# Four transformer stages on one core: the order of turns, output transposes and depooling statistics in the first attention

## The reference

```
# first attention (16 heads of 8), per batch
Q = heads(LN(x)) * 8 ** -0.5;  K, V = heads(ctx[..., :128]), heads(ctx[..., 128:])
logits = Q @ K.T + b + (-1e12) * invalid
x = x + tanh(g_xattn[0]) * softmax(logits) @ V
...
# depooling of the second layer, from ctx and the patch lengths alone
h_patch = rmsnorm(ctx)[..., :128];  s[t] = a * s[t-1] + bcoef * h_patch[t]
depool_out = s[plug],  plug = clip(cumsum(boundary_mask) - 1, 0, 127)
```

## Time and profile before

| | us |
|---|---|
| median of three runs | 1140.29 (1137.04 to 1141.31) |
| the profiled execution | 1144.96 |
| its span | 1143.6 |
| PE busy in the span | 924.6 (81%) |
| DVE busy | 663.6 (58%) |
| ACT busy | 439.8 (38%) |
| GpSimd busy | 438.5 (38%) |
| mean granted TensorE clock | 0.876 of full |

### The profile page before, as it was taken

How to read it: one execution, slowest core, us unless ns; L and a number is a source line. 1 busy time by engine, 2 the same in 40 slices (tenths; PEclk the granted TensorE clock), 3 DMA queues, 4 the chain that set the end, 5 groups by cost and what they waited for, 6 DMA issues and landing times.

```text
span 1143.6 us, 23576 instructions
## 1 busy us (share of the span) xinstructions
PE 924.6 (81%) x8435; PEld 736.0 (64%) x8435; DVE 663.6 (58%) x1745; ACT 439.8 (38%) x864; POOL 438.5 (38%) x718
## 2 busy tenths in 40 slices
PE   2867795999982988995777859999577878888898
PEld 2545674888872766774556648888546666666565
DVE  3787644776775555433354525756655776642655
ACT  0444534333322232330444315566404454554312
POOL 5444444443620544325465443647233453100100
PEclk9999757999995999997899659999756999996999
DMA  5321112121213000002122111123111010000262
GB/s 173 103 52 53 56 48 85 37 43 48 65 41 104 14 12 12 1 1 67 57 71 67 34 26 47 43 59 77 33 33 39 25 27 21 13 7 29 74 192 86
DMA packets 51310, 59.34 MB, mean 52 GB/s; under 512 B 7456, under 2 KB 36928, under 8 KB 50816
## 3 DMA queue, kind: packets, MB, share of 16 engines
q1 hardware_dynamic: 45776, 46.44, 13.7%
q0 software_dynamic: 4992, 10.23, 4.1%
q10 hardware_dynamic: 432, 1.18, 0.3%
HBM read 42.81 MB, written 9.24 MB: 46 GB/s over the span
## 4 chain that ended last, share of the span: by engine, by line
PE 59%; DVE 19%; issue 6%; DMA 6%; POOL 4%; ACT 3%; SPq 2%; POOLq 0%; DVEq 0%; ACTq 0%
PE banks L412 9%; DVE NM L482 6%; PE banks L420 4%; PE bank L181 4%; PE banks L175 3%; PE banks L176 3%; PE banks L177 3%; PE banks L1805 3%; PE bank L433 3%; PE bank L2227 3%; PE banks L1806 3%; PE banks L1807 3%; PE banks L1808 3%; PE bank L2118 2%; DMA QT<-NMT 2%
## 5 line engine op out<-in xcount | busy, mean ns | idle before, releaser
L412 PE MATMUL banks<-KT,QT 31*128 31x128 f32 (+1 forms) x1280 | 158.4, 381 | 90.9 <-DVE NM L482 43.6
L482 DVE TENSOR_REDUCE NM<-banks 128x4 f32<-128x1024 f32 (+1 forms) x112 | 136.7, 1221 | 141.3 <-PE banks L412 141.2
L412 PEld LDWEIGHTS banks<-KT,QT 31*128 31x128 f32 x1280 | 111.0, 219 | 123.6 <-DVE NM L482 53.2
L456 ACT ACTIVATE EE<-banks 128x1024 f32<-128x1024 f32 x112 | 114.8, 1025 | 191.9 <-PE banks L420 191.9
L420 PE MATMUL banks<-QT,KT 32*128 32x128 f32 x1792 | 157.4, 319 | 2.9 <-ACT EE L456 2.5
L420 PEld LDWEIGHTS banks<-QT,KT 32*128 32x128 f32 x1792 | 130.0, 216 | 7.9 <-issue 6.6
L1737 POOL DMA_INDIRECT XG<-xn,SL x92 | 89.4, 972 | 103.5 <-PE bank L1775 84.4
L433 PE MATMUL bank<-EE,VV 128*32 128x128 f32 x1792 | 73.5, 311 | 0.8 <-ACT EE L456 0.8
L1874 ACT ACTIVATE ONE<-CP,EC 128x128 fp32r<-128x128 f32 x92 | 37.0, 403 | 81.1 <-PE bank L2057 56.9
L433 PEld LDWEIGHTS bank<-EE,VV 128*32 128x32 f32 x1792 | 53.1, 124 | 12.6 <-issue 8.4
L175 PE MATMUL banks<-HH,W1H 128*128 128x512 f32 x128 | 51.7, 404 | 6.5 <-DVE HH L2583 6.2
(11 more groups left out here) (404 smaller groups left out, 2423.2 us busy)
## 6 DMA issues: line engine op xcount, KB each, us to landing
RAW<-in_w SPq DMA_DIRECT2D x19, 512.0 KB, 3.8
CBS<-cw SPq DMA_DIRECT2D x32, 256.0 KB, 3.6
ys<-Y SPq DMA_DIRECT2D x92, 64.0 KB, 1.5
RAW<-in_w SPq DMA_DIRECT2D x8, 352.0 KB, 3.1
KT<-in_keys SPq DMA_DIRECT2D x8, 256.0 KB, 3.0
KT<-KQ SPq DMA_DIRECT2D x32, 64.0 KB, 1.9
QT<-KQ SPq DMA_DIRECT2D x32, 64.0 KB, 1.9
CTX<-in_ctx SPq DMA_DIRECT2D x3, 512.0 KB, 6.4
```

The costliest lines, as they stand in the source:

```text
L412: ins = pe.matmul(out, self.QT[r, b1 % 4, 128 * g:128 * g + 128], moving(r, 128 * g), start=True, stop=True)
L456: act.activation(self.EE[:, b % 2, 2 * p:2 * p + 2, :].rearrange("p i k -> p (i k)"), self.K.SB[:, :], ACT.Exp).then_inc(sig("ee").sem, 1)
L482: dve.tensor_reduce(out, src, AX.X, ALU.max, negate=True).then_inc(sig("m1").sem, 1)
```

## The change

In `pe`, scores 0 come ahead of the turn of x, and the turn of the outputs comes right behind scores 1, ahead of the depooling matmul and the router. In `act`, exp 0 comes ahead of the copy QC. In `dve`, the start of a depooling group keeps the masks and two of the four bn_stats; the other two, the four aggregates and the two tiny operations become a function of their own, called one step later between the two maxima. In `pool`, the power goes to that later step.

```diff
@@ pe
+            H.pe_scores(0, b1, moving, b3, keys)
             if s < NBAT:
...
                 pe.transpose(A[:, 0:128], self.XN[:, s % 2, :], K.ident).then_inc(sig("x_turned").sem, 1)
                 read_a = [sig("qcc")(s + 1)]
-            H.pe_scores(0, b1, moving, b3, keys)
...
             H.pe_scores(1, b1, moving, b3, keys)
+            if 0 <= b4 < NBAT:
+                for r in read_a:
+                    pe.wait_ge(*r)
+                H.pe_out(b4, A)
+                read_a = [sig("on")(b4 + 1)]
             g, part = self.stage(s - 1)
...
             read_b = self.early.pe(s, read_b)
-            if 0 <= b4 < NBAT:
-                for r in read_a:
-                    pe.wait_ge(*r)
-                H.pe_out(b4, A)
-                read_a = [sig("on")(b4 + 1)]
@@ act
+            if 0 <= b3 < NBAT:
+                H.act_exp(b3, 0)
             if s < NBAT:
                 act.wait_ge(*sig("x_turned")(s + 1))
...
                 act.copy(self.QC[:, s % 2, :], A[:, 0:128]).then_inc(sig("qcc").sem, 1)
-            if 0 <= b3 < NBAT:
-                H.act_exp(b3, 0)
@@ dve
+            g, part = self.stage(s - 1)
+            if 0 <= g < NGRP and part == 0:
+                self.dve_depool_stats(g)
             if 0 <= b1 < NBAT:
                 H.dve_max(b1, 1)
-            g, part = self.stage(s - 1)
@@ dve_depool_start
-        for i, (b, c) in enumerate(cols):
+        for i, (b, c) in enumerate(cols[0:2]):
             dve.bn_stats(st[:, 8 + 6 * i:14 + 6 * i], K.CTX[:, b, :]).then_inc(*dv.up())
-        for i, (b, c) in enumerate(cols):
-            dve.wait_ge(dv.sem, dv.n - 3 + i)
+
+    def dve_depool_stats(self, g):
+        K, sig, dve, dv = self.K, self.K.sig, self.K.nc.vector, self.K.dv
+        st, rs = K.ST[:, 4, :], K.RS[:, 4, :]
+        for i in range(2, 4):
+            dve.bn_stats(st[:, 8 + 6 * i:14 + 6 * i], K.CTX[:, 4 * g + i, :]).then_inc(*dv.up())
+        dve.wait_ge(*dv.now())
+        for i in range(4):
             ins = dve.bn_aggr(st[:, 2 * i:2 * i + 2], st[:, 8 + 6 * i:14 + 6 * i])
@@ pool
-            g, part = self.stage(s)
+            g, part = self.stage(s - 1)
             if 0 <= g < NGRP and part == 0:
                 pool.wait_ge(*sig("dep_ms")(g + 1))
```

## The result

The changed kernel took 1126.7 us, the median of four runs (1125.48 to 1127.6), beside 1140.8 us of the kernel before on the same chip (1137.04 to 1149.11); the ratio is 0.986, interval 0.9817 to 0.9902. The forecast was 1132.2 with a range from 1127 to 1141. The sign was right, the size was 5.5 us short, and the time lies just outside the range.

What follows compares the result with a forecast made beforehand. Each step was taken as one loop through TensorE and VectorE, with VectorE nearly always late. Terms -2.4 - 4.3 + 1.6 - 1.5 + 1.0 - 0.2 - 2.3 = -8.1 us gave 1132.2 us against the median, range 1127 to 1141.

Steps and rivals of the forecast that it cites:

- The split: Statistics moved off VectorE's tail into the next step's gap at s = 4, 7, 10: -2.4 us.
- The marks named ahead: Expected in the trace: ON's wait under 1 us, aggregates between maxima with gap near 2.9 us, phase end near 170.
- the signs of being wrong: Low clock in more stretches, X and UU over 0.6 us more often, scores half 0 waiting outside s = 8, 12.
- clock term (-0.2 us): TensorE's clock in the steps: one fall more, +0.8 us, and one less, -1.0 us; net -0.2 us.
- The outputs' turn: Turn ahead of depooling matmuls and router on TensorE: VectorE's ON stops waiting for it, -4.3 us.
- The price of 1.6 us on the other side: Sums end about 0.4 us after the second maximum at s = 4, 7, 10, 13: +1.6 us.
- The split covers it: At s = 5, 8, 11 the split's later second maximum hides the later counts: 0, against 1.2 us uncovered.
- The x turn: x turned behind scores half 0 on TensorE: 2.6 us gained, 1.1 lost to ScalarE's order; net -1.5 us.
- The late exp: At s = 12 ScalarE's router normalization delays the exp that scores half 1 needs: +1.1 us, between 0 and 1.65.
- the two mask rows: At s = 7, 11 they delay the row of maxima by 2.80 us of issue; scores half 0 wait, costed at 0.
- Port meetings: VectorE's X meets GpSimd's weight subtraction on shared ports, three meetings more: +1.0 us.
- End of the phase: From s = 16: router's list matmul finds its rows, last turn comes sooner at s = 19; -0.9 and -1.4, -2.3 us.

Runs made afterwards that it cites:

- e2: Kernel before with only the statistics split and the power on GpSimd moved; 1160.52 us, ratio 0.9923.
- d1: Kernel before with two unneeded 128x384 matmuls in TensorE's pause ahead of scores 1 in steps 4 to 16; 1142.14 us, ratio 1.002.
- e1: Kernel before with only the outputs' turn moved right behind the second scores; 1161.68 us, ratio 0.9954.
- e4: Changed kernel without the statistics split, so with both reorders on TensorE and the one on ScalarE; 1156.68 us, ratio 0.9896 to the kernel before.
- f1: Changed kernel with unneeded 128x384 matmuls, three in step 15 and six in step 16; 1130.45 us, ratio 0.989 to the kernel before.
- f2: As f1, with two more unneeded matmuls in each of steps 17 and 18; 1132.03 us, ratio 0.989 to the kernel before.
- f4: As f1, with two more unneeded matmuls at the end of TensorE's part of the phase; 1160.97 us, ratio 0.9939 to the kernel before.

## Why the prediction was right and wrong

**The phase as a whole.** The sum came out: 8.1 us forecast; 7.6 in the first pair of traces, and 8.3 between the means of two traces of before (177.5) and four of after (169.2). That is partly luck, since the terms didn't: the split gave more than twice its share, and the two turns ahead of s = 16 next to nothing. The marks named ahead are there, the phase near 170 among them, but for the gap of the maxima at s = 8, which is 3.95 us and not near 2.9. Of the signs of being wrong, one showed plainly: the low clock stands in stretches that were full before (60.0 to 63.4 us, and from 128 us on). Scores half 0 waited for queries at s = 4 too, by 0.39 us.

**The split.** Mis-sized: 2.4 us forecast, 6.5 alone and 5.2 as the last part added. The reckoning of VectorE's work holds by the steps of e2 (1.0 to 1.3 us shorter three times, 0.4 to 0.5 longer), and the gap of the maxima came out at 2.98 us at s = 5 where near 2.9 was forecast. What it left out are the falls of the clock at s = 9 and 12, 1.6 and 2.1 us in the first trace of before, which e2 doesn't have. The prediction's clock term (-0.2 us) named s = 6, 8 and 9 and not the half clock from 113.5 to 120.2 us at s = 12. That TensorE at full clock makes these steps as short as this is shown by d1 (7.82 and 6.17 us with no split). That the split is what keeps the clock up there is argued, from one trace each.

**The outputs' turn.** The gain of 4.3 us was right as a wait that goes, and wrong as time that comes: counts, sums and scores took it back. The price of 1.6 us on the other side had 0.4 at each of the four sums, where 0.25 each were measured, and nothing at the counts, where e1 has 2.4 us more, mostly two of 1.5 us at the half clock. "The split covers it" held in the whole change (1.0 us at the counts, two times), and without the split it didn't.

**The x turn.** Forecast -1.5 net. Alone it costs 3.6 us, in the whole change its 0.3 us can't be told from nothing. The waits of 1.22 and 1.20 us went as forecast, and in the first trace of after three others of 2.0 us in all stand at s = 7, 8 and 10. The late exp was there: TensorE waits 0.82 us for it at 115.74, and VectorE is idle 1.47 us at 116.94. So were the two mask rows, 6.1 us of TensorE's wait. They were costed at nothing, since scores half 0 would "end 1 us or more before DVE is ready", and at s = 8 this was wrong in three of the four traces: the first maximum waits 0.57, 0.81 and 0.80 us, and the clock falls behind TensorE's wait of 3.4 us. The prediction had that wait splitting the pause; it was the pause.

**Port meetings.** Forecast +1.0 for three more of them. The mechanism is real, the number isn't: ahead of the first maximum of s = 16 VectorE's instructions that overlap a subtraction on GpSimd take in sum 3.4 and 3.2 us beyond the median of their kind in the two traces of before, and 2.6, 3.9, 3.6 and 2.6 in the four of after (added up from the timelines). Meetings moved and didn't multiply; the prediction took one from the trace of before, which has four. X at 124.27 took 1.34 us and ended 0.15 us behind the subtraction. The Trainium skill, page SBUF — State Buffer, section "SBUF: two separate sides", has an instruction of VectorE with two inputs in SBUF and one of GpSimd that reads SBUF exclude each other: whichever starts first has the ports for its whole length. The trace agrees as to the end: X ends 0.15 us behind the subtraction at 124.27 and at 55.02 alike, though 1.19 and 0.82 us of it were left when X began.

**Clock.** The added fall at s = 6 came (2.66 us pause at 59.81, 1.59 us idle at 61.76). The fall at s = 8, which was to go, stayed in this trace (0.50 from 74 to 77 us) and is missing in the second trace of after; one stood at s = 9 (1.76 us at 87.49); and the one at s = 12, which the prediction didn't have, went, in a step that takes 5.71 us instead of 8.26. A pause of 2.66 us at s = 6 stands in the second trace of after too, with no fall behind it. That falls move from trace to trace of one kernel was not foreseen.

**End of the phase.** Forecast -2.3, measured -2.6: from the first maximum of s = 16 to the phase's end it is 32.1 us in six traces with the early turn and no added matmuls (31.1 in the seventh, e4), and 34.6 to 34.9 without it. Of all the terms it is the one that comes out nearly alike in each combination and as forecast.

**Behind the phase.** This is the step that failed: the sum of the phase, 8.1 us, was taken over to the whole time as though all behind the phase moved along unchanged, with no term and no range for it. In its place stood 10.2 us in the first pair of traces, of which 1.5 come with the change and most of the rest comes and goes from trace to trace. TensorE's timeline right behind the phase, before and then after:

```profile
182.32 0.45 PE L1775 MATMUL bank<-CP,XG 128*128 128x128 f32 x1 [8.51 <-DMA XG<-xn,SL]
...
193.57 0.33 PE L1775 MATMUL bank<-CP,XG 128*128 128x128 f32 x1 [1.40 <-DVE XL L1787]
```

```profile
174.55 0.45 PE L1783 MATMUL bank<-CP,XG 128*128 128x128 f32 x1 [5.38 <-DMA XG<-xn,SL]
...
186.03 0.33 PE L1783 MATMUL bank<-CP,XG 128*128 128x128 f32 x1 [0.52 <-DVE XL L1795]
```

In the whole change TensorE's work ends nearer to XG's landing (a pause of 5.38 us instead of 8.51), and the half clock then lasts until 183.0 us, 8.5 us into the next matmuls; before, it lasts until 188.5, 6.2 us into them, and falls again at 195.2. The following pause is 0.52 us instead of 1.40, and no second fall comes. From the bias's copy (L1724 before) to VectorE's fourth Y (L1942) it is 27.37 us before and 25.88 after: 1.5 us. The stretch takes 25.8 to 25.9 in all four traces of the changed kernel and 27.3 to 27.7 in the seven traces without the early outputs' turn, so it comes with the change. The early turn alone doesn't ensure it: e4, f1, f2 and f4 have it and take 27.2 to 27.5. In the traces whose second pause was read, it is 0.26 to 0.74 us where the stretch is short and 0.84 to 1.68 us where it is long. What sets the clock's return is open; the length of the pause for XG alone doesn't (f4).

The rest comes and goes. Around 1030 us (stretch, length, busy, clock): the first trace of before, then of after, then the second trace of after.

```profile
1024.00:1032.00 8.00, 6.79 (x81) 5.41 (x81) 1.79 (x5) 5.23 (x9) 0.00 (x0) 0.76 0.01 2
1032.00:1040.00 8.00, 8.00 (x76) 6.74 (x78) 0.89 (x3) 2.64 (x3) 0.00 (x0) 0.50 0.00 0
```

```profile
1024.00:1032.00 8.00, 6.08 (x88) 4.94 (x84) 1.38 (x4) 2.35 (x4) 0.00 (x0) 0.79 0.01 3
1032.00:1040.00 8.00, 5.28 (x23) 4.05 (x24) 3.98 (x15) 5.24 (x10) 2.39 (x6) 0.98 0.33 98
```

```profile
1016.00:1024.00 8.00, 6.78 (x84) 5.67 (x82) 1.44 (x4) 4.10 (x8) 0.00 (x0) 0.71 0.01 2
1024.00:1032.00 8.00, 8.00 (x75) 6.48 (x73) 0.90 (x3) 2.74 (x4) 0.00 (x0) 0.50 0.00 0
```

Matched by instruction, the stretch of some 50 us that ends at 1050 us in after takes 56.0 and 48.4 us in two traces of before, and 49.7, 57.7 and 49.7 in three of after (60.2 in the fourth, on the slower chip). Another one, 551 to 601 us, takes 50.9 and 55.2 before and 50.9, 52.8 and 50.9 after. So 6.3 of the 10.2 us are one low stretch of the clock that the first trace of before happened to have and that of after had not; 1.7 more lie from 700 to 750 us, where the second trace of before is as short as after. With the 1.5 us above that leaves 0.7.

The four comparisons give 0.986, 0.994, 0.9861 and 0.9937. In the three of them in which the kernel before takes 1141 us, all runs together (single runs of either kernel spread by 15 us and more) have a mean of 1142.4 us over 42 runs before and 1131.2 us over 18 after, a difference of 11.2 us, give or take 2.9. The phase's 8.3 and the 1.5 behind it are 9.8, within that. The first four times lie at the low end of the changed kernel's own spread, 1125.5 to 1140.9 us, and that put the median outside the range, by 0.3 us: bad luck, as the good sum of the phase was in part good luck.

**The range.** It took in the unknowns of the phase and had no term for the scatter of the time behind it. The medians of two later comparisons, 1134.27 and 1128.12, lie within it, and 0.9937 of 1140.29 would be 1133.1.

**A better kernel.** None shown. With unneeded matmuls in steps 15 and 16 the phase ends 1 to 8 us sooner in single traces, not all of it by them, and the ratio isn't told apart from the changed kernel's (0.989 beside 0.9861, and 0.9907 beside 0.9937).

## What to carry to other kernels

In a loop between two engines the price of an edit isn't only its work: ask what it does to the clock of the steps around it, since a fall cost its step 1.2 to 2.1 us here, as much as the edit itself. Pauses of 1.6 to 3 us had a fall behind them in some traces and none in others, so price such a pause as a range. A wait that goes is not yet time won: see who stands next in the same loop, and try a part beside the others, not alone, as two moves that are each useless or harmful alone may be neutral together. Where the time of a long program scatters by 1 per cent, read an edit's effect from a mark at the end of its own stage, in more than one trace, and put the scatter of the rest into the range.

## What the runs showed of the hardware

The kernel before took 1140.8 to 1141.7 us in three comparisons and 1166.6 and 1169.9 in two others, on other chips. The phase itself is alike (it ends at 168.50 in the changed kernel on a slower chip, and at 168.84 to 170.45 on the others). The difference lies in stretches far behind: the first trace of before and the one with three unneeded matmuls on a slower chip, matched by instruction, differ by 2 us from 250 to 300 us, 2.7 in the next 50, and 13 between 750 and 801. There, 760 to 850 us, TensorE's wait for VectorE's Y is 1.9 us in the kernel before:

```profile
PE bank L2118 <- DVE Y L1942: 1.9, 3, 0.8
```

and in the changed kernel on the slower chip (1.9 on the others):

```profile
PE bank L2126 <- DVE Y L1950: 8.5, 7, 2.9
```

Its cause was not examined; a change must be compared on one chip.

From 140 to 155 us TensorE shows busy for the whole 15 us in the changed kernel and the clock stays at 0.50. Full busy time in the profile did not bring the clock back here, while with nine more matmuls of 128x384 in steps 15 and 16 it was up (0.51 to 1.00 from 128 to 140 us, 0.50 to 0.66 behind). In all four traces of kernels with these matmuls the clock is full up to 144 us or later.
